# One plain fp32 matmul in place of three fp32r passes in a feed-forward product

## What is computed

```
out    = x @ W.T + b                       # W is 1024 x 1024
scores = x @ gate_w.T + gate_b             # 4 ranks: 8, 16, 32, 64
r      = RANKS[argmax(softmax(scores))]    # the chosen rank's weight is 1
y      = layernorm(x + out + (x @ A[:r].T) @ B[:, :r].T)
```

## Time and profile before

| quantity | value |
|---|---|
| median of 3 executions | 3648.78 us (3645.04 to 3649.35) |
| the profiled execution's own time | 3642.94 us |
| its span, first to last instruction | 3641.2 us |
| TensorE busy | 3481.5 us, 96% of the span |
| granted TensorE clock, mean | 0.988 of full speed |
| feed-forward part | from about 2793 us to the end |

### The profile page before, as it was taken

The page is one execution under the profiler, slowest core; times in us unless marked ns, Lnnn a source line. Parts: engine busy times, 40 slices in busy tenths (PEclk is TensorE's granted clock), DMA queues, the critical chain, the costliest instruction groups (busy, mean ns, idle before and its releaser), DMA issues. The chain is left out here.

```text
span 3641.2 us, 56102 instructions
## 1 busy us (share of the span) xinstructions
PE 3481.5 (96%) x20833; PEld 2190.3 (60%) x20833; DVE 2290.6 (63%) x5375; ACT 1866.5 (51%) x3188; POOL 1431.2 (39%) x435
## 2 busy tenths in 40 slices
PE   5999999999999999999999999999998999999998
PEld 4555555555454554555555555454544899999997
DVE  4577777776777772677777776777762444455444
ACT  2546656665667666546656665667675101111100
POOL 1115444554657556115444554657574101011010
PEclk8999999999999999999999999999998999999999
DMA  2221110001000010221110000000012122121221
GB/s 79 55 61 30 35 48 24 25 24 42 18 19 19 19 41 19 57 62 30 36 48 24 24 24 19 19 19 18 13 58 83 47 69 65 56 69 56 65 69 41
DMA packets 158395, 148.33 MB, mean 41 GB/s; under 512 B 9396, under 2 KB 141492, under 8 KB 156056
## 3 DMA queue, kind: packets, MB, share of 16 engines
q1 hardware_dynamic: 158168, 145.34, 13.5%
HBM read 94.39 MB, written 33.62 MB: 35 GB/s over the span
## 5 line engine op out<-in xcount | busy, mean ns | idle before, releaser
L603 ACT ACTIVATE prob<-ps_s,alibi 128x512 f32<-128x512 f32 (+3 forms) x2119 | 1287.2, 633 | 741.6 <-PE ps_s L895 377.9
L540 POOL TENSOR_TENSOR prob<-prob 128x2048 f32<-128x2048 f32 (+1 forms) x240 | 1047.8, 4369 | 977.7 <-ACT prob L603 977.4
L682 DVE TENSOR_REDUCE mxp<-ps_a 128x1 f32<-128x512 f32 x1536 | 978.5, 682 | 296.0 <-PE ps_a L816 284.2
L816 PE MATMUL ps_a<-wol,qst 97*128 97x512 f32 (+3 forms) x2560 | 954.8, 395 | 37.0 <-DVE mxp L685 17.6
L895 PE MATMUL ps_s<-qst,kexp 97*128 97x512 f32 (+3 forms) x2119 | 862.7, 411 | 44.2 <-ACT prob L603 28.5
L895 PEld LDWEIGHTS ps_s<-qst,kexp 97*128 97x128 f32 x2119 | 399.0, 189 | 563.8 <-ACT prob L603 321.5
L685 DVE CUSTOM_DVE_ANT_0 ps_a<-ps_a,maska 128x128 f32<-128x128 f32 (+3 forms) x1024 | 492.4, 507 | 243.8 <-PE ps_a L816 233.3
L828 PE MATMUL ps_o<-prob,val 128*32 128x512 f32 (+3 forms) x5120 | 603.5, 543 | 9.9 <-ACT prob L603 6.6
L816 PEld LDWEIGHTS ps_a<-wol,qst 97*128 97x128 f32 x2560 | 486.5, 194 | 112.7 <-DVE mxp L685 31.9
L1089 POOL TENSOR_TENSOR work<-work,bias_b 128x1024 f32<-128x1024 f32 x32 | 76.9, 2402 | 745.4 <-DVE work L1228 710.9
L828 PE MATMUL ps_sum<-prob,ones 128*32 128x512 f32 (+2 forms) x3072 | 332.5, 505 | 3.7 <-POOL prob L540 3.3
(11 more groups left out here) (129 smaller groups left out, 3994.7 us busy)
## 6 DMA issues: line engine op xcount, KB each, us to landing
wq_raw<-in_L_attn_Wq SPq DMA_DIRECT2D x64, 512.0 KB, 3.5
work<-in_L_attn_hidden_states SPq DMA_DIRECT2D x8, 2048.0 KB, 8.3
qst<-qst SPq DMA_DIRECT2D x64, 256.0 KB
att_scratch<-at_sb SPq DMA_DIRECT2D x64, 256.0 KB, 2.8
at_raw<-att_scratch SPq DMA_DIRECT2D x32, 512.0 KB, 5.2
work<-in_L_attn_hidden_states SPq DMA_DIRECT2D x32, 512.0 KB, 4.1
out<-work SPq DMA_DIRECT2D x32, 512.0 KB, 3.1
work<-in_L_attn_Wo SPq DMA_DIRECT2D x8, 512.0 KB, 4.1
```

The costliest lines, as they stand in the source:

```text
L540: nc.gpsimd.tensor_tensor(even[:, :, c1:], even[:, :, c1:], odd[:, :, c1:], ALU.add).then_inc(pair_done, 1)
L603: nc.scalar.activation(prob[slot_of(steps + k)][:, h, c0:], ps_s[places[GH * (steps + k) + h][0]][:, c0:], ACT.Exp, bias=alibi_of(g, h, k ...
L682: nc.vector.tensor_reduce(top, ps, AX.X, ALU.max).then_inc(a_done, 1)
L816: last = nc.tensor.matmul(ps[:, 0:cols], qst[buf][0:KR, h, t * P:(t + 1) * P], kmax[0:KR, ring(sg):ring(sg) + cols], start=True, stop=True)
```

## The change

`wth` and `wtl` become one tile `wt` in F32, `hth` and `htl` become one tile `ht` in F32. The second product makes one matmul of two F32 operands where it made three of fp32r. VectorE's subtractions for `wtl` and `htl` go away; the one for `btl` stays, in `split_b`. Where TensorE and SyncE waited for the subtractions (`raw_lo`, `htl_done`), they wait for ScalarE's copies (`raw_done`, `ht_done`). The first product and the low-rank product with B keep their passes.

```diff
-        wth = sb(ctx, "wth", [P, DC, WX], F32R)
-        wtl = sb(ctx, "wtl", [P, DC, WX], F32R)
+        wt = sb(ctx, "wt", [P, DC, WX], F32)
-        hth = sb(ctx, "hth", [P, DC, P], F32R)
-        htl = sb(ctx, "htl", [P, DC, P], F32R)
+        ht = sb(ctx, "ht", [P, DC, P], F32)
...
             def load_raw(c):
                 if c in free_at:
-                    sp.wait_ge(raw_lo, free_at[c])
+                    sp.wait_ge(raw_done, free_at[c])
...
-                sp.wait_ge(raw_lo, WORK - 1)
+                sp.wait_ge(raw_done, WORK - 1)
                 load_x(0)
...
                 act.wait_ge(t_ps, START + n + 1)
-                nc.scalar.activation(hth[:], turned(ps_t), ACT.Copy).then_inc(hth_done, 1)
+                nc.scalar.activation(ht[:], turned(ps_t), ACT.Copy).then_inc(ht_done, 1)
...
-            def split_raw(c):
-                dve.wait_ge(raw_hi, c + 1)
-                src = turned(turns[c % 2])
...
+            def split_b():
+                dve.wait_ge(raw_done, RAW)
+                src = turned(turns[(RAW - 1) % 2])
+                nc.vector.memset(btl[RM:2 * RM].bitcast(F32), 0.0)
+                nc.vector.tensor_tensor(btl[0:RM].rearrange("r (o p) -> r o p", p=P), src[0:RM],
+                                        bth[0:RM].rearrange("r (o p) -> r o p", p=P).bitcast(F32),
+                                        ALU.subtract).then_inc(b_lo, 1)
...
                 split_at(1, 1)
                 first_norm(0)
-                for c in range(FIRST, RAW):
-                    split_raw(c)
+                split_b()
...
             def step(n, a, j, has_next, has_after):
-                dve.wait_ge(hth_done, START + n + 1)
-                nc.vector.tensor_tensor(htl[:], turned(ps_t), hth[:].bitcast(F32), ALU.subtract).then_inc(htl_done, 1)
...
             def turn_raw(c):
                 pe.wait_ge(raw_in[raw_at[c]], filled[c])
                 if c >= 2:
-                    pe.wait_ge(raw_lo, c - 1)
+                    pe.wait_ge(raw_done, c - 1)
...
                 for c in range(DC):
-                    nc.tensor.matmul(ps, hth[:, c], wth[:, c, piece(p)], start=c == 0, stop=False,
-                                     skip_group_check=True)
-                    nc.tensor.matmul(ps, hth[:, c], wtl[:, c, piece(p)], start=False, stop=False,
-                                     skip_group_check=True)
-                    last = nc.tensor.matmul(ps, htl[:, c], wth[:, c, piece(p)], start=False, stop=False,
+                    last = nc.tensor.matmul(ps, ht[:, c], wt[:, c, piece(p)], start=c == 0, stop=False,
                                             skip_group_check=True)
...
                 pe.wait_ge(h_done, START + n + 1)
-                pe.wait_ge(htl_done, START + n)
+                pe.wait_ge(ht_done, START + n)
...
-                pe.wait_ge(hth_done, START + n + 1)
-                pe.wait_ge(htl_done, START + n + 1)
+                pe.wait_ge(ht_done, START + n + 1)
...
-                pe.wait_ge(raw_lo, RAW)
+                pe.wait_ge(b_lo, 1)
```

More of the change, by code:

```diff
@@ L23 @@
 LN_PARTS = ("stat", "mean", "var", "root", "inv", "sq", "half", "rstd")
-FF_COUNTS = ["at_in", "ath_done", "atl_done", "x2_in", "y_ps", "y_done", "h_done", "hb_done", "t_ps", "hth_done",
-             "htl_done", "g_ps", "g_vec", "t_done", "l_ps", "tth_done", "ttl_done", "z_ps", "z_done", "o_done",
+FF_COUNTS = ["at_in", "ath_done", "atl_done", "x2_in", "y_ps", "y_done", "h_done", "hb_done", "t_ps", "ht_done",
+             "g_ps", "g_vec", "t_done", "l_ps", "tth_done", "ttl_done", "z_ps", "z_done", "o_done",
              "o_out0", "o_out1"] + [f"ln{i}_{n}" for i in range(2) for n in LN_PARTS]
@@ L961, in feed_forward @@
         raw_buf = [work[:, i] for i in range(WORK)]
-        raw_hi = sem("raw_hi")
-        raw_lo = sem("raw_lo")
+        raw_done = sem("raw_done")
+        b_lo = sem("b_lo")
         raw_ps = sem("raw_ps")
@@ L975, in feed_forward @@
         t_ps = counts["t_ps"]
-        hth_done = counts["hth_done"]
-        htl_done = counts["htl_done"]
+        ht_done = counts["ht_done"]
         g_ps = counts["g_ps"]
@@ L1099, in split_raw @@
                 if c < DC:
-                    nc.scalar.activation(wth[:, :, c * P:(c + 1) * P], src, ACT.Copy).then_inc(raw_hi, 1)
+                    nc.scalar.activation(wt[:, :, c * P:(c + 1) * P], src, ACT.Copy).then_inc(raw_done, 1)
                 elif c == DC:
-                    nc.scalar.activation(wth[:, :, D:WX], src[:, :, 0:RM + NRK], ACT.Copy).then_inc(raw_hi, 1)
+                    nc.scalar.activation(wt[:, :, D:WX], src[:, :, 0:RM + NRK], ACT.Copy).then_inc(raw_done, 1)
                 else:
-                    nc.scalar.activation(bth[:].rearrange("r (o p) -> r o p", p=P), src, ACT.Copy).then_inc(raw_hi, 1)
+                    nc.scalar.activation(bth[:].rearrange("r (o p) -> r o p", p=P), src, ACT.Copy).then_inc(raw_done, 1)
             def split_at(n, par):
@@ L1233, in prologue @@
             def prologue():
-                for c in range(EARLY):
-                    split_raw(c)
                 split_at(0, 0)
-                for c in range(EARLY, FIRST):
-                    split_raw(c)
                 dve.wait_ge(f_c, NRK)
```

## The result

The changed kernel takes 3721.64 us (median of 4, 3718.6 to 3724.83) against 3646.91 us for the kernel before (median of 4, 3642.76 to 3649.35): a ratio of 1.0206, 95% interval 1.0189 to 1.0224, 74.7 us slower.

The account below looks back on a forecast made before the run. TensorE's issued work was taken to bound the loop: +97.5 us for 768 dearer products and -3 at the edges gave +94.5 on 3642.9, so 3737.4, or 3743 us by the median; range 3727 to 3780.

Parts of the forecast that it names:

- The weight loads: Second product: loads stay hidden beside running matmuls and add nothing; if exposed, 0.09 us per instruction, 3871 us, chance 0.07.
- Rival A: Second product: each of four passes takes this loop's 0.166 us, 0.664 a product, +127.5 us, 3774 us in all; chance 0.13.
- C: Second product: each of the two instructions needs only one pass, 0.332 us a product, 3518 us in all; chance 0.04.
- D: Feed-forward loop: something other than TensorE sets the pace, so nothing to measure, 3649 us; chance 0.02.
- the middle between the two ends: Second product: 0.625 us a product, taken between 0.611 and 0.638; 0.127 more than now, +97.5 us over 768 products.
- the lower end: Second product: 0.43 us scaled from 512 to 364 columns, 0.306 an instruction and 0.611 a product.
- the edges: Before the first step and in the last step: removed VectorE subtractions save 2 to 4.5 us together, taken as -3.
- the prologue: Before the first step: transposes and btl wait less on VectorE's subtractions, -1.0 to -2.5 us.
- the end: Last step: second product starts 1.85 us sooner without the exposed htl subtraction, worth -0.9 to -1.85 us.
- the low stretch: Last step: granted clock at 0.50 from 3614.9 to 3621.4 us; if its end stays, the 1.85 us won counts 0.9.

Follow-up runs that it names:

- The streams: The kernel before with matmul streams appended on TensorE after the last step; fp32r passes of 512 columns took 0.233 us with 128 weight columns, 0.231 with 32.

## Why the prediction was off

**What held.** TensorE's instructions set the loop and nothing else did: 857.87 us busy of 857.87, no wait, and a subtraction more or less on VectorE changed nothing. A plain F32 matmul is two instructions of two passes, priced from the attention part's L828: 0.43 x 364/512 = 0.306, and 0.306 was measured in the loop. The weight loads stayed hidden: each takes 0.19 us, all operands use all rows, and L1277 stands at 0.306. The Trainium skill, "TensorE: Matmul & The Clock Gate", Part 3, The mechanism, says in its list that a load overlaps a running matmul only when the row group differs, which neither type bears out here; the same section also lets a load into the background weight buffer run ahead, which would fit, though no run here shows such a buffer. Rival A, four passes of the loop's own 0.166, fell with the same number, although the count of four that the Trainium skill, "FP8 and Floating Point Precision", TensorE Precision Notes, gives fits the two instructions of two passes. C and D fell with the step's length.

**What failed first: the middle between the two ends.** The term was "if every one of the new instructions pays it, it is 0.319 and a product 0.638 [...] so I take the middle, 0.625". The 0.013 us by which an fp32r pass exceeds a pass of L828 was charged to the 128-column weight load beside it, as an unknown. The measured product is 0.612, the lower end: 86.7 us over 768 products where 97.5 were in the sum, 10.8 too many. The streams show why the charge was wrong: fp32r takes nearly as long with weights of 32 columns, and plain F32 takes the same with both. The excess is fp32r's own.

**What failed second: a term that was not there.** The sum priced only the instructions that the change touches, and put the untouched first product at nothing without a reason. The change also moved `ath` and `atl`, and the first product became 0.20 us a step faster, 6.2 us over 31 steps. The pad in the changed kernel took that away again, and 128 bytes gave it to the kernel before.

**What was undersized: the edges.** -3 us was taken, within -2 to -4.5. The table above has -3.5 for the prologue, where -1.0 to -2.5 was the forecast. This stretch varies, so one pair says little of its size: the seven profiled executions with the old prologue have 41.8 to 44.5 us for it, the four with the new one 38.9 to 41.8, and the averages, 43.1 and 39.9, are 3.2 apart. More than the forecast it is either way. The granted clock is part of it, 0.74 on average over the stretch in the kernel before and 0.87 in the changed one.

For the end the table has -0.7, in which the 24 dearer products of the last step, +2.7, are contained: without them it is -3.4 where -0.9 to -1.85 was forecast. The start of the product was right, 1.91 for 1.85. The other 1.5 us are the clock: in the kernel before it was 0.50 for the product's first 3.4 us (3618.21 to 3621.59, the low stretch of the earlier trace rows), in the changed kernel it was 1.00 from the product's start on. The prediction assumed that the low stretch would stay. That it did not is luck as far as these runs tell: with the subtraction back the low stretch was there, and with the pad, where the product also starts early, it covers the product's first 5.8 us and the tail is 31.5 us. Both edges together are -6.9 with the products taken out, 3.9 more than the sum had.

Together: 94.5 - 10.8 - 6.2 - 3.9 = 73.6, and 73.1 was found in the feed-forward part, 74.7 by the medians. The range's lower end took the product at its cheapest and the edges at their best, and had no width for the untouched matmuls; with their 6.2 us it would have reached down to 3721, where the result lies.

## What to carry to other kernels

Before replacing k passes of fp32r by plain F32, compare k passes of the measured fp32r distance with two instructions of twice columns/2.4 ns each; here three passes won by 0.113 us a product, and against four of them, 0.664 us, the plain form at 0.612 would have gained. Price a stream by the distance from start to start of the nearest kind of instruction in the trace, and where two ends remain, look for a reason that one of them must hold before taking the middle. When a change alters the size of a tile, everything allocated behind it moves, so put a pad of the same size in (or price the move) before comparing, and in an fp32r kernel try the places modulo 256 bytes: a pad costs a few hundred bytes, though it paid only in the feed-forward part here.

## What the runs showed of the hardware

- In streams on TensorE alone, the time of an fp32r pass of 512 columns depends on the distance between weights and moving operand modulo 256 bytes: 0.227 us at 0 and 16 bytes, 0.231 to 0.234 from 32 to 160, 0.229 at 192. The feed-forward loop follows this; the projection of the queries in the attention part, at a distance of 0, does not (0.234 and 0.231).
- At its best place an fp32r pass of 512 columns is 0.227, a bf16 one 0.217, and one pass of a plain F32 instruction 0.215 (half of 0.430). The Trainium skill, "TensorE: Matmul & The Clock Gate", Back-to-back issue gap, gives columns/2.4 plus 2.5 ns for an isolated matmul, 216 ns at 512 columns, and 131 ns for one in a stream of loads and matmuls. The bf16 stream, in which every matmul has its own load, stands at the first of the two, and so does a plain instruction with twice the columns (1024/2.4 + 2.5 = 429 ns); no stream here comes near 131 ns, and the fp32r ones lie above both.
- A plain F32 instruction costs 0.114 us at 128 moving columns and 0.110 at 64, and an fp32r pass 0.110 at 128, each with weights of 128 columns: from 128 moving columns down, fewer of them gained nothing here.
- The attention part, same code, ended anywhere within 16 us in ten profiled executions (2788.7 to 2804.6). A difference of two single executions of this kernel says little below that; the windows of the changed part say much more.
